# A selective-scan block on one core: which engine copies out the last states of the staged pairs

## The chip, the core and the metric

The kernel runs on one core of one Trainium2 chip. The metric is the time of one execution on the device in microseconds (us), and the smaller it is the better. The engines are called by their names in the profile: PE is TensorE, DVE is VectorE, ACT is ScalarE, POOL is GpSimd and SP is SyncE. PEld is the weight load of TensorE.

## The reference

A Mamba block and then a mixture of experts work on 8 x 1024 tokens of width 256, both on layer-normed inputs with residual sums. The part that matters here is the selective scan: 512 channels, each with 16 states, and a first-order recurrence over time for each of them.

```python
def step(s, inp):
    d_t, B_t, C_t, u_t = inp
    dA = jnp.exp(d_t[..., None] * A)
    dBu = d_t[..., None] * B_t[:, None, :] * u_t[..., None]
    s = dA * s + dBu
    y_t = jnp.einsum('bdn,bn->bd', s, C_t)
    return (s, y_t)
s0 = jnp.zeros((Bsz, Di, N), dtype=u.dtype)
_, ys = lax.scan(step, s0, xs)
```

After it the top 2 of 8 experts are applied to each token and the result is layer-normed. All values are fp32.

## The kernel before, in words

The first part of the kernel (to about 1785 us of the trace) is the Mamba block with the routing, the second part the experts. Only the first is touched.

**Tiling.** The 8192 tokens are 16 chunks (NC) of 512 tokens (CH). A sequence of 1024 tokens is two chunks, so an even chunk starts its states at zero and the odd chunk behind it starts them from the last states of the even one. The 512 channels are four groups (G) of 128 partitions, and each group has 16 states (N). One scan is one instruction on DVE over 128 channels x 512 tokens for one state n. A chunk is thus 64 scans (SG), which the code counts as steps: step s of a chunk is group s // 16, state s % 16. Every engine has its own loop over the same steps, written out by hand, with tables that say at which step a projection, a routing piece or a copy is issued. Each engine runs its queue strictly in order and semaphores join the queues.

**One scan.** ACT makes the decay, an exp of 128x512 (`exp_a`, line 1215, the most frequent ACT instruction). POOL makes the drive of two states at once (`times_b`, line 902), except for state pairs 2 and 5 (`BMS`), where PE makes it (line 1508) and ACT writes the exp to `dbu`. DVE scans (line 763).

**Held and direct states.** States with n % 3 == 0 are *held*: their exp goes to the fifth PSUM bank, and their result goes to the SBUF tile `ss` (the profile calls it `area`, since it is a part of a larger tile). `ss` has two slots, each for one *staged* pair: states 0 and 3, 6 and 9, 12 and 15. So there are three staged pairs in each group, numbered s = 3t + j over all groups t (`STAGED` holds the first state of each). POOL weighs a staged pair by C (`weigh` of POOL, line 919) and PE adds it up. The other ten states are *direct* pairs; their scans stay in PSUM, DVE weighs them (line 775) and PE adds them up.

**Last states.** In even chunks the last column of each scan goes to the tile `carry`, from which the odd chunk starts. The five direct pairs are copied by ACT (`keep`, line 1222). Before the change the three staged pairs are copied by POOL (line 913), just before it weighs the pair. There are 8 even chunks x 4 groups x 3 pairs = 96 such copies of 128x2.

**What waits for what.** The exp of a held state waits until the scan of the held state before it is done (they share a bank), and the exp of a direct state waits for DVE's weighing of an earlier pair and, in even chunks, for that pair's `keep`. The scan of a staged pair s waits until POOL has weighed pair s - 2, which lay in the same slot. In every chunk, DVE's `add_dt` of group 2 (line 735) stands at step 10 and waits for ACT's `soft_log` (line 1184), which stands at step 12 of ACT's queue; between them at step 9 ACT has the gate's Silu with two table loads (line 1199). A second Silu stands at step 41 (line 1193).

Of the kernel before, what the change touches and what calls it, by code (L numbers as in the profile page):

```python
# [178 lines left out]
def mamba_block(nc, both, x_t, x1_t, b_dram, ln_g, ln_b, W_in, conv_w, conv_b, W_xproj, W_dt, b_dt, A_log, D_param,  # L179
# [29 lines left out]
    with ExitStack() as ctx:  # L209
# [3 lines left out]
        def sem(name):  # L213
            return ctx.enter_context(nc.semaphore(name))
# [85 lines left out]
        wd_turned = sem("turned_dve")  # L300
        wp_turned = sem("turned_pool")
        carry_act = sem("carry_act")
        carry_pool = sem("carry_pool")
        gated = sem("gated")
        made = sem("masks_made")
        lnr_step = sem("routed_ln_step")
# [47 lines left out]
        SCATTER_END = NC * G * HB + 1  # L354
        DIAGONALS = (54, 57, 61, 63)
        DRIVE = (4, 4, 10, 10)
        KEEP_EARLY = (4, 9)
        EARLY_AT = [CUTS[0] * SG + at for at in (47, 48, 50, 51)] + [(CUTS[0] + 1) * SG + at for at in range(46, 54)] + [
            c * SG + 47 for c in CUTS[1:]]
# [85 lines left out]
        def kept(k):  # L445

            c, g, n = k // SG, k // N % G, k % N
            return ND * (G * (c // 2) + g) + product(n) + 1

        def routed(q, j):  # L450

# [159 lines left out]
        def _(dve):  # L611
# [126 lines left out]
            def scan(c, g, n):  # L738
                t = c * G + g
                k = t * N + n  # L740
                if n // 2 in BMS:
                    dve.wait_ge(tb_done, driven(t, n))
                elif n % 2 == 0:
                    dve.wait_ge(dbu_done, products(t, n // 2))
                dve.wait_ge(exp_done, k + 1)
                if held(n):

                    s = 3 * t + n // 6
                    if n in STAGED and s >= 2:
                        dve.wait_ge(wp_done, s - 1)  # L750
                    dst = ss[:, s % 2, n // 3 % 2, :]
                else:
                    dst = ps_a[:, bank(k), :]
                init = 0.0
                if c % 2:
                    init = carry[:, g, n:n + 1]
                    if held(n):
                        dve.wait_ge(carry_pool, 3 * (G * (c // 2) + g) + n // 6 + 1)
                    else:
                        dve.wait_ge(carry_act, kept(k))  # L760
                pair = ps_a[:, bank(k), :], dbu[:, k // 2 % NBU, n % 2, :]
                decay, drive = reversed(pair) if n // 2 in BMS else pair
                dve.tensor_tensor_scan(dst, decay, drive, init, ALU.mult, ALU.add).then_inc(scan_done, 1)  # L763
# [82 lines left out]
        def _(pool):  # L846
# [58 lines left out]
            def weigh(t, j):  # L905

                c, g = t // G, t % G
                n = STAGED[j]
                rows = slice(n, n + 4, 3)
                s = 3 * t + j  # L910
                pool.wait_ge(scan_done, t * N + n + 4)
                if c % 2 == 0:
                    pool.tensor_copy(carry[:, g, rows], ss[:, s % 2, :, CH - 1]).then_inc(carry_pool, 1)
                if s >= 2:
                    pool.wait_ge(wp_turned, s - 1)
                if g == 0:
                    for m in {n // 2, (n + 3) // 2}:
                        pool.wait_ge(c_in[m], 16 * (c + 1))
                pool.tensor_tensor(wp[:, s % 2], ss[:, s % 2], cc[:, rows, :], ALU.mult  # L919
                                   ).then_inc(wp_done, 1)  # L920
# [40 lines left out]
        def _(act):  # L961
# [262 lines left out]
            def follows(k):  # L1224

                return next(j for j in range(k + 1, k + N) if bank(j) == bank(k))

            keep_at = {}
            for t in range(NC * G):
                if t // G % 2 == 0:  # L1230
# [60 lines left out]
            for at in range(STEPS):  # L1291
                c, s = divmod(at, SG)
                if s == HALO_AT and c + 1 < NC:
                    set_halo(c + 1)
                if s == XL_AT and 0 < c < NC:
                    residual_base(c - 1)
                if at == XL_LAST:
                    residual_base(NC - 1)
                for kind, g, q in empty_at.get(at, ()):
                    if kind == "dt":  # L1300
                        soft_abs(q, g)
                    else:
                        empty(kind, g, q)
                for kind, g, q in empty_at.get(at - 1, ()):
                    if kind == "dt":
                        soft_exp(q, g)
                for kind, g, q in empty_at.get(at - 2, ()):
                    if kind == "dt":
                        soft_log(q, g)
                if s in TAPS_ACT and c + 1 < NC:  # L1310
                    tap_product(c + 1, (3, 0, 1, 2)[TAPS_ACT.index(s)])
                if s == SILU_U and c + 1 < NC:
                    silu_u(c + 1)
                    act.preload_act_table_set("natural_log_exp_and_others")
                q = due(at, SILU_Z, 1)
                if q is not None:
                    silu_gate(q)
                    act.preload_act_table_set("natural_log_exp_and_others")
                for j, offset in enumerate(INV_STD):
                    q = due(at, offset, 2)  # L1320
                    if q is not None:
                        inv_std(q, j)
                for j, offset in enumerate(STATS_X1):
                    q = due(at, offset, -1)
                    if q is not None and q < NC - 1:
                        stats_x1(q, j)
                for j, offset in enumerate(INV_STD_X1):
                    q = due(at, offset, -1)
                    if q is not None and q < NC - 1:
                        inv_std_x1(q, j)  # L1330
                if s in NORM and c + 2 < NC:
                    normalise(c + 2, range(2) if s == NORM[0] else range(2, NT))
                if s in XN and 0 < c < NC:
                    normalise_x1(c - 1, range(2) if s == XN[0] else range(2, NT))
                for j, offset in enumerate(EXP_W):
                    q = due(at, offset, -1)
                    if q is not None and q < NC - 1:
                        weight_exp(q, j)
                for j, offset in enumerate(START_DIAGONALS):
                    if at == offset:  # L1340
                        diagonals(0, 2 + j)
                for j, offset in enumerate(DIAGONALS):
                    q = due(at, offset, 1)
                    if q:
                        diagonals(q, j)
                for k, offset in enumerate((IDS_0, IDS_1)):
                    q = due(at, offset, -1)
                    if q is not None and q < NC - 1:
                        row_meta(q, k)
                if c < NC:  # L1350
                    for k in keep_at.get(at, ()):
                        keep(k)
                    exp_a(c, s // N, s % N)

        @block.tensor
# [995 lines left out]
```

## Time and profile before

| | |
|---|---|
| median of 3 runs | 2302.48 us (2300.59 to 2304.11) |
| profiled execution, its own time | 2301.22 us |
| its span, first to last instruction | 2299.4 us |
| TensorE clock granted, mean | 0.971 of full speed |
| busy share of PE, DVE, ACT, POOL | 92%, 88%, 73%, 86% |

The shares are means over both parts of the kernel; in the scan part DVE is busier than in the experts. An "idle before" in a timeline row, in square brackets, is the time that the engine stood still ahead of that row and what ended it.

### The profile page before, as it was taken

The numbers are of one execution on the slowest core, as the hardware profiler recorded it, in microseconds if no ns is written. First come the engines' busy times: TensorE is split into PE (matmuls) and PEld (weight loads), VectorE is DVE, ScalarE is ACT, GpSimd is POOL, SyncE is SP. The second block draws the span as 40 slices with busy tenths as digits, with TensorE's granted clock in tenths as the row PEclk, the third lists the DMA queues.
The fourth block names the chain that finished last, engine by engine and source line by source line (L and its number), as shares of the span: only waits on it lengthen the run. The fifth ranks groups of instructions, "written<-read, shape, count | busy, mean of one in ns | idle before, by whom it ended". The sixth has DMA issues, their size and how long they took to land. (4 is left out here: it accounts for less than half of the span.)

```text
span 2299.4 us, 45508 instructions
## 1 busy us (share of the span) xinstructions
PE 2116.1 (92%) x13263; PEld 1725.8 (75%) x13263; DVE 2034.8 (88%) x2843; ACT 1685.7 (73%) x3447; POOL 1971.4 (86%) x1252
## 2 busy tenths in 40 slices
PE   8889899999989898989898989999978999999996
PEld 5667677777767676767777777777767899999885
DVE  5999999999999999999999999999999556657776
ACT  6787879788888888877778787888765444445664
POOL 3988999999999899989899999989898467667775
PEclk9999999999999999999999999999998999999998
DMA  5041414233241415050514142323325667657886
GB/s 189 3 157 47 148 52 152 68 126 110 86 141 56 165 37 173 23 174 27 168 39 156 52 146 71 130 91 104 102 84 181 135 125 156 131 97 165 182 181 153
DMA packets 226007, 263.59 MB, mean 115 GB/s; under 512 B 101123, under 2 KB 182563, under 8 KB 225636
## 3 DMA queue, kind: packets, MB, share of 16 engines
q1 hardware_dynamic: 175172, 208.07, 29.0%
q0 software_dynamic: 29904, 34.77, 8.3%
q10 hardware_dynamic: 20688, 17.85, 2.5%
q8 instruction: 111, 1.82, 0.3%
q14 instruction: 132, 1.08, 0.2%
HBM read 196.75 MB, written 71.71 MB: 117 GB/s over the span
## 5 line engine op out<-in xcount | busy, mean ns | idle before, releaser
L902 POOL TENSOR_TENSOR dbu<-drive_u,w_all 128x1024 f32<-128x1024 f32 x384 | 904.1, 2365 | 61.2 <-DVE ps_a L763 43.4
L1215 ACT ACTIVATE ps_a<-delta,a_neg 128x512 f32<-128x512 f32 x768 | 518.4, 685 | 117.8 <-DVE area L763 103.0
L919 POOL TENSOR_TENSOR wp<-area 128x1024 f32<-128x1024 f32 x192 | 453.2, 2360 | 8.5 <-DVE area L763 7.8
L775 DVE TENSOR_TENSOR wd<-ps_a,area 128x1024 f32<-128x1024 f32 x320 | 383.0, 1197 | 0.0
L1481 PEld LDWEIGHTS ps_y<-ident,wd 128*128 128x128 f32 x2560 | 309.3, 146 | 97.7 <-issue 72.1
L1481 PE MATMUL ps_y<-ident,wd 128*128 128x128 f32 x2560 | 347.1, 282 | 13.0 <-DVE wd L775 13.0
L2064 POOL DMA_INDIRECT acc_scratch<-ow,e_meta x135 | 221.2, 1639 | 132.8 <-DVE ow L1975 122.7
L1508 PEld LDWEIGHTS ps_a<-dg,duT 128*128 128x128 f32 x2048 | 255.1, 201 | 67.0 <-issue 65.0
L1508 PE MATMUL ps_a<-dg,duT 128*128 128x128 f32 x2048 | 265.5, 285 | 38.3 <-ACT carry L1222 36.0
L2306 PEld LDWEIGHTS e_ps_h<-xT,w_tile 128*128 128x128 f32 x2160 | 259.6, 192 | 16.9 <-DVE xT L1953 10.5
L2306 PE MATMUL e_ps_h<-xT,w_tile 128*128 128x128 f32 x2160 | 265.5, 276 | 2.7 <-DVE xT L1953 1.9
L2316 PE MATMUL e_ps_o<-area,e_hT 128*128 x1080 | 255.6, 379 | 0.4 <-DVE e_hT L1960 0.4
L763 DVE TENSOR_TENSOR_SCAN area<-ps_a,carry,dbu 128x512 f32<-128x512 f32 x192 | 242.0, 1260 | 1.5 <-issue 1.5
L763 DVE TENSOR_TENSOR_SCAN ps_a<-ps_a,carry,dbu 128x512 f32<-128x512 f32 x192 | 237.6, 1271 | 0.4 <-issue 0.4
L763 DVE TENSOR_TENSOR_SCAN area<-ps_a,dbu 128x512 f32<-128x512 f32 x192 | 230.4, 1200 | 5.2 <-ACT ps_a L1215 5.0
L763 DVE TENSOR_TENSOR_SCAN ps_a<-ps_a,dbu 128x512 f32<-128x512 f32 x192 | 225.9, 1211 | 4.9 <-ACT ps_a L1215 4.9
L1491 PE MATMUL ps_y<-ident,wp 128*128 128x128 f32 x1536 | 215.1, 286 | 9.6 <-POOL wp L919 9.5
L2316 PEld LDWEIGHTS e_ps_o<-area,e_hT 128*128 128x128 f32 x1080 | 194.9, 190 | 21.7 <-issue 0.8
L2113 ACT ACTIVATE e_hT<-e_ps_h,b_turned 128x128 f32<-128x128 f32 x270 | 84.9, 364 | 170.9 <-PE e_ps_h L2306 167.3
L1491 PEld LDWEIGHTS ps_y<-ident,wp 128*128 128x128 f32 x1536 | 187.2, 149 | 23.0 <-POOL wp L919 14.1
L2105 ACT COPY w_tile<-w_all 128x1024 f32 x135 | 141.0, 1045 | 57.6 <-issue 51.5
L1389 PE MATMUL ps_p<-area 128*128 128x512 f32 x368 | 178.0, 593 | 0.8 <-ACT area L1096 0.8
(248 smaller groups left out, 3842.1 us busy)
## 6 DMA issues: line engine op xcount, KB each, us to landing
area<-b_scratch SPq DMA_DIRECT2D x128, 512.0 KB, 4.8
w_all<-b_scratch SPq DMA_DIRECT2D x96, 512.0 KB, 3.9
dg<-xs_scratch SPq DMA_DIRECT2D x540, 32.0 KB
area<-in_L_attn_x_dram SPq DMA_DIRECT2D x32, 512.0 KB, 4.9
ee<-acc_scratch SPq DMA_DIRECT2D x32, 512.0 KB, 4.0
x_scratch<-area SPq DMA_DIRECT2D x16, 512.0 KB, 2.9
acc_scratch<-area SPq DMA_DIRECT2D x16, 512.0 KB
area<-x_scratch ACTq DMA_DIRECT2D x32, 256.0 KB
```

What stands on the lines that cost most here:

```text
L763: dve.tensor_tensor_scan(dst, decay, drive, init, ALU.mult, ALU.add).then_inc(scan_done, 1)
L775: dve.tensor_tensor(wd[:, s % NWD], states(k, 2), cc[:, n:n + 2, :], ALU.mult).then_inc(wd_done, 1)
L902: pool.tensor_tensor(dbu[:, k % NBU], du[:, g % 2, :].unsqueeze(1).broadcast_to([P, 2, CH]), bb[:, row:row + 2, :], ALU.mult).then_inc(dbu ...
L919: pool.tensor_tensor(wp[:, s % 2], ss[:, s % 2], cc[:, rows, :], ALU.mult).then_inc(wp_done, 1)
L1215: act.activation(dst, dl[:, g, :], ACT.Exp, scale=a_neg[:, g, n:n + 1]).then_inc(exp_done, 1)
L1389: ins = pe.matmul(dst, taps[:, g, k, :], xin[:, g, k:k + CH], start=(k == 0), stop=(k == TAPS - 1))
L1481: ins = pe.matmul(ps_y[:, i, :], wd[:, s % NWD, h, i * P:(i + 1) * P], ident[:], start=False, stop=False, is_transpose=True, skip_group_ch ...
L1491: ins = pe.matmul(ps_y[:, i, :], wp[:, s % 2, h, i * P:(i + 1) * P], ident[:], start=False, stop=(j == 2 and h == 1 and i == NT - 1), is_t ...
L1508: ins = pe.matmul(ps_a[:, bank(k), i * P:(i + 1) * P], duT[:, i, :], dg[:, p, h, i, :], start=True, stop=True)
L2064: pool.indirect_dma_start(out=acc_dram, out_offset=bass.IndirectOffsetOnAxis(ap=meta[:, old, 1:].bitcast(U32), axis=0), in_=ow[:, old, :], ...
L2306: ins = pe.matmul(inner(1 - par, j), w1s[:, 1 - par, k, j * P:(j + 1) * P], xT[:, 1 - par, :, k, :], start=(k == 0), stop=(k == KD - 1))
L2316: ins = pe.matmul(ps_o[:, par, 0:D], hT[:, par, k, :], w2[:, bass.ds((e * KF + k) * D, D)], start=(k == 0), stop=(k == KF - 1))
```

## The change

ACT copies out the last states of the three staged pairs, instead of POOL. The copy of the pair that starts at state n is issued at step n + 6 of the same group (for n = 12 that is step 2 of the next group), ahead of that step's exp. A new semaphore `carry_held` takes the place of `carry_pool`. The scan that writes a slot of `ss` again, two staged pairs later, now waits for ACT's copy too, since POOL's weighing no longer implies it.

```diff
-        carry_pool = sem("carry_pool")
+        carry_held = sem("carry_held")
...
+        KEEP_HELD = 6
...
+        def copied(s):
+            return 3 * (G * (s // (3 * G) // 2) + s // 3 % G) + s % 3 + 1
...
                     if n in STAGED and s >= 2:
                         dve.wait_ge(wp_done, s - 1)
+                        if (s - 2) // 3 // G % 2 == 0:
+                            dve.wait_ge(carry_held, copied(s - 2))
...
                     if held(n):
-                        dve.wait_ge(carry_pool, 3 * (G * (c // 2) + g) + n // 6 + 1)
+                        dve.wait_ge(carry_held, 3 * (G * (c // 2) + g) + n // 6 + 1)
...
                 pool.wait_ge(scan_done, t * N + n + 4)
-                if c % 2 == 0:
-                    pool.tensor_copy(carry[:, g, rows], ss[:, s % 2, :, CH - 1]).then_inc(carry_pool, 1)
...
+            def keep_held(s):
+
+                t, n = s // 3, STAGED[s % 3]
+                act.wait_ge(scan_done, t * N + n + 4)
+                act.copy(carry[:, t % G, n:n + 4:3], ss[:, s % 2, :, CH - 1]).then_inc(carry_held, 1)
+
+            held_at = {s // 3 * N + STAGED[s % 3] + KEEP_HELD: s for s in range(3 * NC * G) if s // (3 * G) % 2 == 0}
...
                     for k in keep_at.get(at, ()):
                         keep(k)
+                    if at in held_at:
+                        keep_held(held_at[at])
                     exp_a(c, s // N, s % N)
```

In the rows below a name in square brackets is a semaphore: `scan_done` and `weighed_dve` come from DVE, `carry_act` from ACT's `keep`, `proj_full` from PE. The lines of the changed kernel stand four or more further down (1215 becomes 1219, 1222 becomes 1226, 1136 becomes 1140); the new copy is line 1236.

**ACT, start of an even chunk.** This is ACT's queue of the kernel before from step 3 to the first table load of step 9 of chunk 6:

```order
963 L1215 ACTIVATE ps_a<-delta,a_neg 128x512 [waits scan_done]
964 L1215 ACTIVATE dbu<-delta,a_neg 128x512 [waits scan_done] x2
965 L1091 ACTIVATE area<-ps_p,lnb,lng 128x512 [waits proj_full]
966 L1215 ACTIVATE ps_a<-delta,a_neg 128x512 [waits scan_done]
967 L1222 COPY carry<-ps_a 128x2 [waits weighed_dve]
968 L1215 ACTIVATE ps_a<-delta,a_neg 128x512 [waits carry_act,weighed_dve] x2
969 L1136 COPY area<-ps_p 128x4x128 [waits proj_full]
970 L1199 ACT_TABLE_LOAD [waits proj_evacuated1,proj_evacuated0]
```

The same place in the changed kernel reads:

```order
1003 L1219 ACTIVATE ps_a<-delta,a_neg 128x512 [waits scan_done]
1004 L1219 ACTIVATE dbu<-delta,a_neg 128x512 [waits scan_done] x2
1005 L1095 ACTIVATE area<-ps_p,lnb,lng 128x512 [waits proj_full]
1006 L1236 COPY carry<-area 128x2 [waits scan_done]
1007 L1219 ACTIVATE ps_a<-delta,a_neg 128x512 [waits scan_done]
1008 L1226 COPY carry<-ps_a 128x2 [waits weighed_dve]
1009 L1219 ACTIVATE ps_a<-delta,a_neg 128x512 [waits carry_act,weighed_dve] x2
1010 L1140 COPY area<-ps_p 128x4x128 [waits proj_full]
1011 L1203 ACT_TABLE_LOAD [waits proj_evacuated1,proj_evacuated0]
```

The copy of states 0 and 3 stands ahead of the exp of step 6 and waits on `scan_done`, as that exp does; the exp does not wait for the copy.

**ACT, start of an odd chunk.** This is ACT's queue of the changed kernel from step 1 to step 5 of chunk 5; the kernel before has the same rows without line 1236:

```order
851 L1219 ACTIVATE ps_a<-delta,a_neg 128x512 [waits carry_act,weighed_dve]
852 L1140 COPY area<-ps_p 128x4x128 [waits proj_full]
853 L1104 COPY area<-ps_p 128x512 [waits proj_full]
854 L1236 COPY carry<-area 128x2 [waits scan_done]
855 L1219 ACTIVATE ps_a<-delta,a_neg 128x512 [waits carry_act,weighed_dve]
856 L1095 ACTIVATE area<-ps_p,lnb,lng 128x512 [waits proj_full]
857 L1219 ACTIVATE ps_a<-delta,a_neg 128x512 [waits scan_done]
```

Here the copy is the one of states 12 and 15 of the last group of the even chunk ahead, at step 2.

**POOL.** This is POOL's queue of the kernel before in the first groups of an even chunk:

```order
198 L913 COPY carry<-area 128x2
199 L919 TENSOR_TENSOR wp<-area 128x1024
200 L889 TENSOR_TENSOR drive_u<-delta,xc 128x512
201 L902 TENSOR_TENSOR dbu<-drive_u,w_all 128x1024
202 L876 DMA xs_scratch<-area,sli 67456x258
203 L902 TENSOR_TENSOR dbu<-drive_u,w_all 128x1024 x2
204 L913 COPY carry<-area 128x2
205 L919 TENSOR_TENSOR wp<-area 128x1024
```

In the changed kernel the two rows of line 913 are gone, and nothing else on this queue has moved.

## Rows read from the trace of the kernel before

**Rows 1.** The page, part 1: busy time of each engine, share, instructions.
```profile
PE 2116.1 (92%) x13263; PEld 1725.8 (75%) x13263; DVE 2034.8 (88%) x2843; ACT 1685.7 (73%) x3447; POOL 1971.4 (86%) x1252
```

**Rows 2.** Busy time of each engine in a 200 us window of the scans.
```profile
400.00:600.00 200.00, 185.56 (x1154) 143.88 (x1153) 194.97 (x215) 166.84 (x348) 189.65 (x112) 0.98 0.33 112
```

**Rows 3.** Waits of DVE, 110 to 1760 us: total us, times, longest.
```profile
DVE delta L735 <- ACT delta L1184: 22.9, 15, 1.8
DVE ps_a L763 <- PE ps_a L1508: 13.1, 15, 1.6
```

**Rows 4.** Waits of POOL, the same stretch, the longest.
```profile
POOL dbu L902 <- DVE ps_a L763: 41.1, 43, 2.4
```

**Rows 5.** The tile carry: POOL's copies, duration in ns min/median/max.
```profile
L913 POOL COPY carry<-area x96: 177/192/250, 50.6 to 1673.7; 128x2 f32<-128x2 f32 x96
```

**Rows 6.** Timeline of ACT: small copies and what starts behind them.
```profile
578.28 0.20 ACT L969 ACTIVATE area<-area 128x12 uint32<-128x12 uint32 x1
578.38 0.56 ACT L1100 COPY area<-ps_p 128x512 f32<-128x512 f32 x1
...
584.75 0.17 ACT L1222 COPY carry<-ps_a 128x2 f32<-128x2 f32 x1
584.79 1.35 ACT L1215 ACTIVATE dbu<-delta,a_neg 128x512 f32<-128x512 f32 x2
```

**Rows 7.** Timeline of chunk 6, ACT and then DVE.
```profile
694.09 0.69 ACT L1215 ACTIVATE ps_a<-delta,a_neg 128x512 f32<-128x512 f32 x1
694.75 0.16 ACT L1222 COPY carry<-ps_a 128x2 f32<-128x2 f32 x1
695.01 1.30 ACT L1215 ACTIVATE ps_a<-delta,a_neg 128x512 f32<-128x512 f32 x2
696.25 0.57 ACT L1136 COPY area<-ps_p 128x512 f32<-128x512 f32 x1
...
693.53 1.19 DVE L775 TENSOR_TENSOR wd<-ps_a,area 128x1024 f32<-128x1024 f32 x1
...
707.38 0.69 DVE L735 SCALAR_TENSOR_TENSOR delta<-ps_p,delta 128x512 f32<-128x512 f32 x1 [1.75 <-ACT delta L1184]
```

**Rows 8.** ACT at step 9 of chunks 4 and 14, first and last of four.
```profile
482.73 0.59 ACT L1136 COPY area<-ps_p 128x512 f32<-128x512 f32 x1 [0.48 <-PE ps_p L1450]
...
1571.24 0.59 ACT L1136 COPY area<-ps_p 128x512 f32<-128x512 f32 x1 [0.47 <-PE ps_p L1450]
```

**Rows 9.** Timeline of chunk 5 at step 9, ACT and then PE.
```profile
586.70 1.92 ACT L1215 ACTIVATE ps_a<-delta,a_neg 128x512 f32<-128x512 f32 x3
588.68 0.59 ACT L1136 COPY area<-ps_p 128x512 f32<-128x512 f32 x1
...
588.01 0.63 PE L1450 MATMUL ps_p<-ident,area 128*128 128x128 f32 x4 [0.70 <-DVE area L785]
```

**Rows 10.** Timeline at step 41 of chunk 4, ACT and then DVE.
```profile
535.36 1.07 ACT L1120 COPY area<-ps_p 128x512 f32<-128x512 f32 x2 [0.18 <-PE ps_p L1405]
...
538.97 0.19 DVE L643 TENSOR_REDUCE mx<-ps_p 128x4 f32<-128x32 f32 x1 [0.38 <-PE ps_p L1413]
```

**Rows 11.** Timeline of DVE, chunk 0 at step 9.
```profile
60.17 1.22 DVE L763 TENSOR_TENSOR_SCAN area<-ps_a,dbu 128x512 f32<-128x512 f32 x1 [1.84 <-ACT ps_a L1215]
```

**Rows 12.** Windows at step 41 of chunks 2 and 4; DVE's wait in chunk 2.
```profile
324.00:326.00 2.00, 2.00 (x11) 2.00 (x10) 1.97 (x5) 1.99 (x4) 1.34 (x1) 0.50 0.01 4
539.00:541.00 2.00, 2.00 (x18) 1.73 (x17) 2.00 (x4) 1.97 (x3) 0.87 (x2) 1.00 0.00 0
...
330.98 2.34 DVE L763 TENSOR_TENSOR_SCAN ps_a<-dbu,ps_a 128x512 f32<-128x512 f32 x2 [1.59 <-PE ps_a L1508]
```

**Rows 13.** Timeline of POOL at one copy, and DVE's scan beside it.
```profile
521.19 0.18 POOL L913 COPY carry<-area 128x2 f32<-128x2 f32 x1
521.33 2.35 POOL L919 TENSOR_TENSOR wp<-area 128x1024 f32<-128x1024 f32 x1
...
520.22 1.20 DVE L763 TENSOR_TENSOR_SCAN area<-ps_a,dbu 128x512 f32<-128x512 f32 x1
```

## The prediction, made before the changed kernel ran

> **What bounds the kernel now.** I read the page first. PE has the largest share and POOL 86%, with 1971.4 us [rows 1]; that alone would say that work taken off POOL is worth something. But the shares are means over two parts, so I then took the windows of the scan part. In 200 us of it DVE is busy 194.97 us, POOL 189.65, PE 185.56 and ACT 166.84 [rows 2]. DVE stands still about 5 us, and the question is only what ends those waits. The list of DVE's waits from 110 to 1760 us answers it: 22.9 us, 15 times, for ACT's `soft_log` of line 1184, and 13.1 us, 15 times, for a drive made by PE (line 1508) [rows 3]. No wait of DVE in that list is ended by POOL. The list of POOL's waits shows the opposite direction: POOL stands 41.1 us in 43 places for DVE's scans, at the drives of line 902 alone [rows 4]. So POOL is nearly full, but it follows DVE; DVE is the bound, and where DVE waits, the end of the wait comes out of ACT or PE.
>
> The timelines show the two chains behind those waits. In every chunk DVE stands at `add_dt` of group 2, for 1.75 us in chunk 6 [rows 7]. What it waits for is ACT, which from step 3 on runs without a gap through exps, copies, Silu and two table loads. A longer ACT queue ahead of that point makes DVE's wait longer, unless ACT itself has a gap on the way. So the price of the change is decided by where the 96 copies fall against ACT's gaps, and not by ACT's 73%.
>
> **What the change removes.** POOL loses 96 copies with a median of 192 ns [rows 5], 18.4 us of busy time. The next instruction starts 0.14 us behind a copy's start (521.19 to 521.33) [rows 13], so its queue is 96 x 0.14 = 13.4 us shorter. DVE never waits for POOL [rows 3], and what POOL gains becomes a longer wait for DVE's scans in the places of [rows 4]. Gain: 0. The cover is DVE itself; if it went, the gain would be up to 13.4 us.
>
> **What the change adds to ACT.** 96 copies from SBUF of two elements. The trace has no such copy on ACT, so I bound it by three rows. An SBUF to SBUF operation of 12 elements takes 0.20 us and the next one starts 0.10 us behind its start [rows 6]: this is nearest, and I take c = 0.10. The cheapest is a `keep` with nothing behind it that waits for it, 0.04 us (584.75 to 584.79) [rows 6]. The dearest is a `keep` between two exps of which the second waits for it: from exp to exp 694.09 to 695.01 is 0.92 us [rows 7], and two exps without it are 0.62 apart (from 695.01, two exps and then line 1136 at 696.25 [rows 7]), so 0.30. The rows of the new order show that the exp behind the new copy has no wait on it, which is why I don't take 0.30, but it stays the upper end.
>
> The copy's own wait is free. At steps 6 and 12 it waits for the scan for which that step's exp waits anyway, and at step 2 of the next group it waits for the last scan of the group, for which the exp of step 0 has waited already. No ACT instruction is held by a wait that it did not have.
>
> **What the change adds to DVE.** The scan of staged pair s waits for the copy of s - 2. That copy stands in ACT's queue four to six steps ahead of this scan's own exp, and the scan has always waited for that exp. So the wait is over before it is reached: 0.
>
> **Which of the copies count.** A copy costs time only where ACT runs from it to one of DVE's waits without a gap. Twelve copies fall in each even chunk; I go through the places.
> - Chunks 2, 6 and 8, step 6: no gap to `soft_log`. But the `keep` behind it starts at 694.75, when DVE's weighing ends (693.53 + 1.19 = 694.72), which is 0.66 us behind the exp ahead instead of 0.62 [rows 7]. That slack of 0.04 takes a part: 3 x (0.10 - 0.04) = 0.18 us.
> - Chunks 4, 10, 12 and 14, step 6: ACT stands 0.48 or 0.47 us at step 9 for PE (line 1450) [rows 8]. The copy disappears in it: 0, also at 0.30.
> - Odd chunks (8 of them), step 2: three exps start at 586.70, so ACT could start line 1136 at 586.70 + 3 x 0.62 = 588.56, and it starts at 588.68 because PE's transposes end at 588.01 + 0.63 = 588.64 [rows 9]. They hang on DVE's gate. The slack is 0.12: 0, and at 0.30 it is 8 x 0.18 = 1.4 us.
> - Chunk 0, step 6: DVE waits 1.84 us for ACT behind the table loads [rows 11], without slack: 1 x 0.10.
> - Steps 34 and 38 of the seven even chunks from 2 on: two copies ahead of the second Silu, and ACT's only gap there is 0.18 us; behind it stands the logit matmul, for which DVE waits 0.38 us [rows 10]. 7 x (0.20 - 0.18) = 0.14 us.
> - The other copies are followed by one of ACT's waits for a DVE scan before anything of DVE's depends on them: 0.
>
> Sum: 0.18 + 0 + 0 + 0.10 + 0.14 = **0.4 us slower**. With c = 0.04 it is 0 + 0 + 0 + 0.04 + 0 = 0.04, and with c = 0.30 it is 3 x 0.26 + 1.4 + 0.3 + 7 x 0.42 = 5.4 us.
>
> The sum stands against the profiled execution's own time, 2301.2 + 0.4 = 2301.6 us. That execution is 1.3 us below the median of the three runs, so for the median I forecast 2302.48 + 0.4 = **2302.9 us**. About 0.2% (4.6 us) is what a measurement of this kernel can tell from no change.
>
> **The rivals.**
> - *POOL's relief counts.* If POOL's lateness reached DVE in a way that the waits don't show, up to 13.4 us would go: 2289 us. For it speaks that POOL is 189.65 of 200 us busy [rows 2]. Against it, that no wait of DVE ends with POOL [rows 3] and that POOL waits so often itself [rows 4]. A second way is contention in SBUF: if DVE stood for as long as POOL's copies take, 18.4 us would go, 2284 us. The scan that wholly contains a copy (520.22 to 521.42, the copy at 521.19) takes 1.20 us [rows 13], and the scans with a zero start take 1.19 to 1.22 in the rows that I read, copy or not. Together 0.07.
> The Trainium skill has a rule that speaks for this rival: GPSIMD Engine Reference, Specifications, says that GpSimd's SBUF interfaces are shared with VectorE and that instructions with two SBUF inputs contend. By that rule a scan or a weighing here is not such an instruction, as its names in the rows give one input in PSUM (`ps_a`) and one in SBUF, and the trace agrees, with 1.20 us beside a copy.
> - *The copy drains ACT.* Slower: each copy costs the whole bracket of 0.30 us at the places above. The result would be +5.4 us, 2307.9 us. It passes 0.2% from c = 0.27 on (26c - 2.4 = 4.6, with 3 + 8 + 1 + 14 = 26 copies and 2.4 us of slack). For it speaks the `keep` at the same step, which does cost that; against it, that nothing waits for the new copy, and the 0.04 of the `keep` at 584.75 [rows 6]. 0.07.
> - *The clock falls elsewhere.* In chunks 2, 6, 8 and 14, but not in 4, 10 and 12, DVE waits another 1.6 us at step 42 (1.59 in chunk 2), and there the granted TensorE clock is 0.50 (its 1.2 GHz level) just before, against 1.00 (2.4 GHz) in chunk 4, though PE is busy in both [rows 12]. A shift of some tenths may move that: from 4 x 1.6 = 6.4 us faster to 3 x 1.6 = 4.8 us slower, 2296.5 to 2307.7 us. The order has little to do with it, so most of this lies within 0.2%. 0.06.
> - *The forecast*: 0.80.
>
> **The numbers.** The forecast's own range is 0.04 to 1 us over before, with the spread of the runs (2300.6 to 2304.1) about it. The range reaches down for some of the clock's cases and up towards the drained copy: 2299.0 to 2307.0 us. Faster by over 0.2%: 0.07, nearly all from the first rival. Slower: 0.08, 0.06 from the drained copy and 0.02 from the clock. Within 0.2%: 0.85.
>
> **What would show it right or wrong.** POOL's busy time should fall by some 18 us to 1953 and its waits for DVE's scans grow by some 13. ACT should have 96 copies at line 1236 with about 0.2 us each, and the next instruction 0.10 us behind. DVE's wait for `soft_log` should stay at 22.9 us to within 1 us, and no wait of DVE should name `carry`. Line 1136 in chunks 4, 10, 12 and 14 should have its idle time of 0.48 cut to about 0.38. I am wrong if DVE's scans or weighings have become shorter than before, if DVE's waits for PE have fallen with POOL's work, or if ACT's copy costs 0.3.

## The result, and the profile after

The changed kernel takes 2302.96 us (median of 20 runs, 2298.16 to 2305.70). The kernel before, run beside it as often, takes 2298.59 us (2293.83 to 2304.11). The ratio is 1.0018, 95% interval 1.0012 to 1.0025: slower by 4.4 us, just under the 0.2% of the prediction. Of the three runs that were known ahead, two (2302.48 and 2304.11) lie above all 17 later ones of that kernel and the third (2300.59) above most. So the forecast of 2302.9 us hit the number by luck: its base was 3.9 us too high, and its step of 0.4 us was 4.0 us too small.

The two profiled executions hide this. They took 2301.22 and 2301.63 us, 0.4 us apart, because single executions of one kernel differ by several us. The busy row after the change answers to [rows 1]:

```profile
PE 2116.6 (92%) x13263; PEld 1725.2 (75%) x13263; DVE 2036.9 (89%) x2843; ACT 1692.9 (74%) x3543; POOL 1957.2 (85%) x1156
```

POOL lost 14.2 us of its 1971.4 and ACT gained 7.2, as wanted. DVE, which should not have changed at all, is busy for 2.1 us more with the same 2843 instructions. The waits from 110 to 1760 us (total, times, longest) answer to [rows 3] and [rows 4]:

```profile
DVE delta L739 <- ACT delta L1188: 22.9, 15, 1.8
DVE ps_a L769 <- PE ps_a L1521: 11.9, 13, 1.6
...
POOL dbu L908 <- DVE ps_a L769: 46.9, 46, 2.4
...
POOL wp L923 <- DVE area L769: 15.7, 19, 2.1
```

DVE's wait for `soft_log` is the same to the tenth, and POOL's waits for DVE have grown (its weighings waited 7.2 us in the kernel before, and its copies 3.6). The list of waits thus doesn't show the loss, and DVE's instructions have to be looked at one by one. One of them stands out. In chunk 10 DVE tests which expert tiles have started, one 128x8 instruction at scan 47. Timelines of POOL and then DVE there, first before the change:

```profile
1209.78 0.19 POOL L913 COPY carry<-area 128x2 f32<-128x2 f32 x1
1209.92 2.36 POOL L919 TENSOR_TENSOR wp<-area 128x1024 f32<-128x1024 f32 x1
1212.25 2.36 POOL L902 TENSOR_TENSOR dbu<-drive_u,w_all 128x1024 f32<-128x1024 f32 x1
...
1210.75 1.39 DVE L621 BATCH_NORM_STATS2 st<-area 128x6 f32<-128x256 f32 x4
1212.06 0.25 DVE L679 SCALAR_TENSOR_TENSOR tile_started<-seen,tile_row,region_base 128x8 f32<-128x8 f32 x1
```

and after it:

```profile
1206.23 2.37 POOL L923 TENSOR_TENSOR wp<-area 128x1024 f32<-128x1024 f32 x1
1208.55 2.36 POOL L908 TENSOR_TENSOR dbu<-drive_u,w_all 128x1024 f32<-128x1024 f32 x1
...
1208.51 2.43 DVE L683 SCALAR_TENSOR_TENSOR tile_started<-seen,tile_row,region_base 128x8 f32<-128x8 f32 x1
```

Before, the test began 0.19 us ahead of POOL's drive and was done in 0.25 us, 0.03 us behind the end of the weighing (1209.92 + 2.36 = 1212.28). After, it began 0.04 us ahead of the drive, 0.09 us before the weighing ended (1206.23 + 2.37 = 1208.60), and it ended at 1210.94, with the drive (1208.55 + 2.36 = 1210.91). Its inputs `seen` and `region_base` are both in SBUF. The batch statistics just ahead have one SBUF input and run beside POOL's weighing without any delay. Chunk 14 shows the same hold, across two POOL instructions (after the change):

```profile
1643.34 2.37 POOL L923 TENSOR_TENSOR wp<-area 128x1024 f32<-128x1024 f32 x1
1645.66 2.36 POOL L908 TENSOR_TENSOR dbu<-drive_u,w_all 128x1024 f32<-128x1024 f32 x1
...
1644.11 3.94 DVE L683 SCALAR_TENSOR_TENSOR tile_started<-seen,tile_row,region_base 128x8 f32<-128x8 f32 x1
```

It ends at 1648.05, POOL at 1648.02. The Trainium skill, SBUF — State Buffer, section SBUF: two separate sides, says that GpSimd and VectorE share one pair of SBUF ports as an exclusive lock, which a VectorE instruction in a 2-port perf mode or with two SBUF inputs needs, and that whichever starts first has it for its whole length. The trace agrees that DVE is shut out, with 3.94 us for 8 elements per partition. By the recorded starts it doesn't show who gets the pair at a change from one POOL instruction to the next, since in chunk 10 the drive got it although the test was issued 0.04 us earlier.

Two inputs are not the whole condition here. In chunk 8 of before a 128x8 instruction with a single SBUF tensor as input is held in the same way, until POOL's drive ends (987.08 + 2.35 = 989.43, against 989.47):

```profile
987.08 2.35 POOL L902 TENSOR_TENSOR dbu<-drive_u,w_all 128x1024 f32<-128x1024 f32 x1
...
986.71 2.76 DVE L685 TENSOR_SCALAR base_full<-region_base 128x8 f32<-128x8 f32 x1
```

In the last experiment it is moved to the start of chunk 0. There it takes 0.16 us in the one kernel, where POOL stands still at that time, and 2.11 us in the other, until POOL's drive ends (45.49 + 2.11 = 47.60, against 45.22 + 2.35 = 47.57). Whether it runs in such a perf mode no run here shows.

The theories to be tested:
- **Port theory**: some DVE instructions are held until POOL's instruction beside them has ended. POOL's queue without its copy of 0.14 us stands differently against DVE. The test in chunk 10 misses its opening and costs 2.2 us.
- **Copy theory**: the 4 us are ACT's time in the 96 copies.
- **Drift theory**: such long durations wander from one execution to the next.

### The profile page after: what moved, and what is told of

Read it like the earlier page. It is cut to its first block and busy times, and to the rows that moved or that the text cites. A ratio compares the mean times of both kernels' runs of the same rounds, so it can differ in the third digit from the quotient of the medians.

```text
span 2299.7 us, 45682 instructions
## 1 busy us (share of the span) xinstructions
PE 2116.6 (92%) x13263; PEld 1725.2 (75%) x13263; DVE 2036.9 (89%) x2843; ACT 1692.9 (74%) x3543; POOL 1957.2 (85%) x1156
```

## A measure with less noise

DVE's waits of 1.1 to 1.6 us for PE's drive, of which the clock rival spoke, do wander: there are 7 and 5 of them in two profiles of before, and 3 to 9 in the others. So for each profile I take DVE's stretch from the `soft_log` wait in chunk 0 to that in chunk 15, and subtract the waits of over 1 us for that drive. I call the rest the *net stage*. Its two ends, before and then after:

```profile
66.64 0.69 DVE L735 SCALAR_TENSOR_TENSOR delta<-ps_p,delta 128x512 f32<-128x512 f32 x1 [2.99 <-ACT delta L1184]
...
1691.81 0.69 DVE L735 SCALAR_TENSOR_TENSOR delta<-ps_p,delta 128x512 f32<-128x512 f32 x1 [0.90 <-ACT delta L1184]
```

```profile
64.73 0.69 DVE L739 SCALAR_TENSOR_TENSOR delta<-ps_p,delta 128x512 f32<-128x512 f32 x1 [1.19 <-ACT delta L1188]
...
1691.22 0.69 DVE L739 SCALAR_TENSOR_TENSOR delta<-ps_p,delta 128x512 f32<-128x512 f32 x1 [0.91 <-ACT delta L1188]
```

Before: 1625.2 less 7 waits of 9.8 us in all is 1615.4. After: 1626.5 less 6 waits of 8.2 is 1618.3. The net stage of a kernel comes from its one profile; two profiles of one kernel differ by 0.4 us (before) and 0.6 us (after), and what wanders ahead of chunk 0's wait is not in it. The table has everything that was measured: the median, the ratio to the kernel before as it ran beside this one (its medians there are 2298.59, 2298.05 or 2297.87, so ratios compare better than medians), the net stage, and the test in chunk 10:

| kernel | median us | ratio (95%) | net stage us | test in chunk 10, us |
|---|---|---|---|---|
| before | 2298.59 | | 1615.4 | 0.25 |
| before again | 2297.28 | 1.0000 (0.9990 to 1.0010) | 1615.8 | 0.26 |
| after | 2302.96 | 1.0018 (1.0012 to 1.0025) | 1618.3 | 2.43 |
| after again | 2302.62 | 1.0016 (1.0007 to 1.0025) | 1618.9 | 2.44 |
| both copies | 2299.55 | 1.0004 (0.9995 to 1.0013) | 1618.2 | 0.27 |
| no copies | 2299.20 | 1.0007 (0.9996 to 1.0017) | 1616.3 | 2.46 |
| ACT's copies twice | 2303.95 | 1.0026 (1.0017 to 1.0035) | 1621.9 | 2.44 |
| copies behind `keep` | 2298.87 | 1.0002 (0.9993 to 1.0010) | 1616.3 | 2.43 |
| after, test of chunk 10 moved | 2299.78 | 1.0005 (0.9996 to 1.0014) | 1615.6 | 0.19 |
| after, four tests moved | 2293.36 | 0.9973 (0.9964 to 0.9983) | 1612.0 | 0.19 |
| before, four tests moved | 2292.86 | 0.9978 (0.9968 to 0.9988) | 1609.8 | 0.20 |
| behind `keep`, four moved | 2291.18 | 0.9973 (0.9963 to 0.9983) | 1609.5 | 0.19 |
| before, all moved | 2287.54 | 0.9957 (0.9943 to 0.9970) | 1605.4 | 0.20 |
| behind `keep`, all moved | 2282.59 | 0.9936 (0.9921 to 0.9950) | 1604.4 | 0.19 |

## The experiments

**Before again.** No edit.

> The kernel before, unchanged, so that a second profiled execution of it exists. Every theory: ratio 1.000 (0.9993 to 1.0007). Port theory (a DVE instruction with two SBUF inputs is held until the GpSimd instruction beside it has ended): in this profile the test of the started tiles in chunk 10, which took 0.25 us in the first profile of before (at 1212.06), again lasts about 0.25 us, because GpSimd comes to the same seam at the same time; in chunks 12 and 14 it lasts 2.7 and 4.1 us as before. Drift theory (such waits and the half-clock waits wander by chance between executions): it lasts 0.2 us in one execution and 2.4 us in another of the same kernel.

Ratio 1.0000. The test lasts 0.26 us again (0.25 in the first profile), and POOL's drive begins 0.18 us behind it:

```profile
1206.28 0.26 DVE L679 SCALAR_TENSOR_TENSOR tile_started<-seen,tile_row,region_base 128x8 f32<-128x8 f32 x1
...
1206.46 2.36 POOL L902 TENSOR_TENSOR dbu<-drive_u,w_all 128x1024 f32<-128x1024 f32 x1
```

Its wandering waits are 5, not 7, and its span is 5.8 us shorter: 3.2 us by these waits and 3.5 us ahead of the net stage, which begins at 63.12 and not at 66.64. So they wander, and the test doesn't.

**After again.** No edit.

> The changed kernel, unchanged, for a second profiled execution. Both theories of a real loss: ratio 1.0018 (1.0010 to 1.0026). Port theory: the test of the started tiles in chunk 10 lasts 2.4 us again (first profile of after: 2.43). Copy theory (what is lost is ScalarE's time in the copies): that instruction may last either 0.2 or 2.4 us and the time is 1.0018 all the same.

Ratio 1.0016, and 2.44 us in the test, with the drive 0.06 us behind it (1210.40 and 1210.46):

```profile
1210.40 2.44 DVE L683 SCALAR_TENSOR_TENSOR tile_started<-seen,tile_row,region_base 128x8 f32<-128x8 f32 x1
...
1210.46 2.36 POOL L908 TENSOR_TENSOR dbu<-drive_u,w_all 128x1024 f32<-128x1024 f32 x1
```

The drift theory falls for the test. The loss is real, since it came out twice.

**Both copies.** The place for `spare` comes from `base_full`, which now shares one with another 128x8 tile; that and the new semaphore are left out here.

```diff
+        spare = sb("spare", [P, 2])
...
+                if c % 2 == 0:
+                    pool.wait_ge(spared, copied(s) - 1)
+                    pool.tensor_copy(spare[:], ss[:, s % 2, :, CH - 1]).then_inc(spared, 1)
                 if s >= 2:
                     pool.wait_ge(wp_turned, s - 1)
```

> The changed kernel, with GpSimd's copies put back beside ScalarE's: GpSimd copies the same two last states per pair into a small spare tile that nobody reads (room for it comes from letting two 128x8 tiles of the tile table share one place). ScalarE's copies stay the ones that are used. Port theory: GpSimd stands against DVE as in the kernel before, the test of the started tiles in chunk 10 falls from 2.43 to about 0.25 us, and the time goes back by about 2.2 us to a ratio of 1.0008 (only ScalarE's own price of 0.4 to 0.6 us, and what is not explained, is left). Copy theory: ScalarE's copies are all still there, so the ratio stays at 1.0018 or above. Third possibility, GpSimd's copies cost something themselves: above 1.0025.

More work than in either kernel, and 3.1 us faster than after again. The test has its opening back: POOL's copy stands at 1209.90, the drive at 1212.36 and the test 0.19 us ahead of it, with 0.27 us:

```profile
1212.17 0.27 DVE L685 SCALAR_TENSOR_TENSOR tile_started<-seen,tile_row,region_base 128x8 f32<-128x8 f32 x1
```

The median supports the port theory. The net stage doesn't: it is that of after (1618.2 against 1618.3 and 1618.9), though the test gave 2.2 us back. Of these, 0.5 us went into four other held instructions in chunks 8, 12 and 14, which are 0.12 to 0.14 us longer each than after the change. I can't place the rest.

**After, four tests moved.**

```diff
-            c * SG + 47 for c in CUTS[1:]]
+            c * SG + 46 for c in CUTS[1:]]
```

> The changed kernel, with the test of the started tiles (one 128x8 instruction on DVE with two SBUF inputs) in chunks 10, 12, 14 and 15 one scan earlier, at scan 46 of the chunk instead of scan 47, where GpSimd sits in the issue of its indirect stores and runs no arithmetic. Port theory: the four instructions fall from 2.43, 2.63, 3.94 and 0.22 us to about 0.2 us each, DVE gets back 8.4 us, of which next to all lies on the path since DVE waits for little there: 2303.0 - 8.4 = 2294.6 us, a ratio to the kernel before of 0.998 (0.9965 to 0.9995). Rival (the long durations are a record of something DVE would wait for anyway, such as the drive of the next scan or the clock): the time goes back into the next wait and the ratio stays at 1.0018.

2293.36 us, 9.6 below after. All four tests take 0.19 to 0.20 us, and 6.3 to 6.9 us of the net stage go (from 1618.3 and 1618.9 to 1612.0). POOL and DVE in chunk 10:

```profile
1204.61 1.01 POOL L882 DMA_INDIRECT xs_scratch<-area,sli  x1 [1.24 <-DVE sli L671]
1205.92 0.96 POOL L882 DMA_INDIRECT xs_scratch<-area,sli  x1 [0.30 <-issue]
...
1205.63 0.19 DVE L683 SCALAR_TENSOR_TENSOR tile_started<-seen,tile_row,region_base 128x8 f32<-128x8 f32 x1
```

The rival, that the time would go back into the next wait, falls for the greater part. The four tests became 8.4 us shorter and the net stage 6.3 to 6.9. In chunk 14 a part came back as a wait, for nothing that the profile names, which neither profile of after has:

```profile
1639.26 1.23 DVE L769 TENSOR_TENSOR_SCAN area<-ps_a,dbu 128x512 f32<-128x512 f32 x1 [1.13 <-issue]
```

**Before, four tests moved.** The same edit in the kernel before.

> The kernel before, with the test of the started tiles in chunks 10, 12, 14 and 15 at scan 46 of the chunk instead of 47. Its four instructions last 0.25, 2.75, 4.07 and 0.22 us in the profiles of before. Port theory: they fall to 0.2 us each, DVE gets back 6.4 us, so 2298.6 - 6.4 = 2292.2 us, ratio 0.9972; what is then left between this kernel and the changed one with the same move (2293.4) is the real price of having the copies on ScalarE rather than on GpSimd, 0 to 1.5 us. Copy theory (the 4 us between after and before are ScalarE's time): this kernel has to come out 4 us below the changed one with the same move, at 2289.4 us, ratio 0.996.

2292.86 us. The copy theory wanted 2289.4 by the median, which did not come; the net stages, 1609.8 and 1612.0, leave 2.2 us between the two kernels where no test is held. By the net stage that is the price of the copies on ACT, more than I had allowed (0 to 1.5). The medians don't show it: they are 0.5 us apart, and the ratios lean the other way (0.9978 and 0.9973), well within their intervals.

**No copies.** The edit takes out line 913 and the scans' wait for it, and adds:

```diff
+            dve.memset(carry[:], 0.0)
```

> The kernel before, without the 96 copies of held last states on any engine: neither GpSimd nor ScalarE makes them, and the scans of those pairs in the odd chunks start from zero, which DVE writes into the tile once at the start. That part of the computation is left out. GpSimd is then as short as in the changed kernel, and ScalarE as short as in the kernel before. Port theory: GpSimd reaches chunk 10 as in the changed kernel, the test of the started tiles there lasts 2.4 us instead of 0.25, and the time is that of the changed kernel less ScalarE's 0.5 to 1 us: ratio 1.0014 (1.0005 to 1.0022), slower than before though work was only taken away. Copy theory: nothing is left that could cost anything, ratio 1.000 or below. Relief theory (GpSimd's copies held the kernel up): 0.994 (13.4 us less).

This kernel leaves out the last states of the staged pairs: those scans start at zero in the odd chunks too. Its ratio is 1.0007 with an interval that holds 1: the median decides nothing. The profile does: POOL without copies, ACT as before, and the test lasts 2.46 us. So it is POOL's missing 0.14 us that makes the test miss, and nothing on ACT. The net stage is 0.5 to 0.9 us over before, not 2.2. DVE gets a part back: four other held instructions are 0.12 to 0.15 us shorter each, as the POOL copy in their way is gone (3.95 against 4.08 in chunk 14), and its other waits are 0.7 us less (30.8 against 31.5). The relief theory falls.

**ACT's copies twice.** `spare` is made as in the kernel with both copies.

```diff
                 act.wait_ge(scan_done, t * N + n + 4)
+                act.copy(spare[:], ss[:, s % 2, :, CH - 1])
                 act.copy(carry[:, t % G, n:n + 4:3], ss[:, s % 2, :, CH - 1]).then_inc(carry_held, 1)
```

> The changed kernel, with each of ScalarE's 96 copies made twice, the first time into a small spare tile that nobody reads. Port theory with a small price of a copy: one more copy of 0.08 to 0.10 us costs what the first does at the places that are not covered, 0.4 to 1.4 us in all, so ratio 1.002 (1.0017 to 1.0025). Copy theory: the 96 copies cost 4 us, so 96 more cost at least 4 us again: ratio 1.0035 or above. The test of the started tiles in chunk 10 stays at 2.4 us by both.

1.0026. The median is 1.0 to 1.3 us over after's and the ratio 0.8 to 1.0 thousandths (1.8 to 2.3 us), at the upper edge of what the port theory had (1.0025) and below the copy theory's 1.0035. The net stage grows by 3.0 to 3.6 us, more than the 0.4 to 1.4 expected. One place shows the price of one copy. At step 26 of the even chunks DVE waits for PE's drive; in chunk 4 of before, after and twice:

```profile
517.97 1.23 DVE L763 TENSOR_TENSOR_SCAN ps_a<-dbu,ps_a 128x512 f32<-128x512 f32 x1 [0.44 <-PE ps_a L1508]
```

```profile
513.97 1.23 DVE L769 TENSOR_TENSOR_SCAN ps_a<-dbu,ps_a 128x512 f32<-128x512 f32 x1 [0.53 <-PE ps_a L1521]
```

```profile
516.12 1.23 DVE L770 TENSOR_TENSOR_SCAN ps_a<-dbu,ps_a 128x512 f32<-128x512 f32 x1 [0.63 <-PE ps_a L1523]
```

0.09 and 0.10 us for each copy, without any cover, at a place that I had put among those that cost nothing. The same wait stands in all seven even chunks from 2 on: 0.44 us in before, 0.53 or 0.54 in after, 0.63 with the copies twice. Chunk 0, which has no such wait in before, has one of 0.37 and 0.56 us in the two profiles of after and of 0.71 us with the copies twice.

**Copies behind `keep`.**

```diff
-            held_at = {s // 3 * N + STAGED[s % 3] + KEEP_HELD: s
+            held_at = {s // 3 * N + STAGED[s % 3] + (7, 7, 5)[s % 3]: s
```

> The changed kernel, with each of ScalarE's copies of held last states behind a copy of last states that ScalarE makes anyway, in one step with it, so that its time lies in the 0.25 us that the next exponential waits for there: pairs 0 and 6 one step later (seven scans after the pair's first), pair 12 one step earlier (five after). Port theory: GpSimd's work is as in the changed kernel, the test in chunk 10 stays at 2.4 us, and only ScalarE's uncovered share goes, 0.4 to 0.6 us: ratio 1.0015 (1.0006 to 1.0022). Copy theory: with the copies hidden the time falls back to that of before, ratio 1.000. Rival to both: two copies in a row drain ScalarE for longer, 1.002 or above.

1.0002, against the 1.0015 that the port theory gave, and the net stage is that of the kernel without copies (1616.3): here the 96 copies cost nothing. The wait at step 26 is 0.44 us again in the seven chunks, and gone in chunk 0. The median is 3.8 to 4.1 us under after's, of which the net stage explains 2.0 to 2.6. (The profiled execution was the slowest of the twelve, 2307.08 us, with 9 of the wandering waits.) The port theory alone was wrong about this, and the ratio is the one that the copy theory gave: where the copies stand on ACT is about as large a part of the loss as the test.

**After, test of chunk 10 moved.**

```diff
-            c * SG + 47 for c in CUTS[1:]]
+            c * SG + 47 - (c == 10) for c in CUTS[1:]]
```

> The changed kernel, with the test of the started tiles one scan earlier in chunk 10 alone; in chunks 12, 14 and 15 it stays at scan 47. It lasts 2.43 us in chunk 10 in the profiles of after. Port theory: 0.2 us in chunk 10, 2.6 and 3.9 us in chunks 12 and 14 as before, chunk 10 itself takes 106.5 to 106.8 us from its wait for delta to the next one's instead of 108.8, and the time falls by about 2.2 us, to a ratio of 1.0008 (1.0000 to 1.0015). Copy theory: the copies are all there and 1.0018 stays.

2299.78 us, 2.8 to 3.2 under after, and chunk 10 takes 106.7 us instead of 108.8. That shows what this one instruction costs: 2.1 us there.

**Behind `keep`, four tests moved.** The last two edits together, the tests in all four chunks.

> Both moves that helped by themselves: ScalarE's copies behind the copies of last states that it makes anyway, and the test of the started tiles in chunks 10, 12, 14 and 15 at scan 46. If ScalarE's copies cost time only by where they stand, the scan stage without its half-clock waits is that of the kernel before with the same move of the test (1609.8 us from chunk 1 to chunk 15), against 1612.0 in the changed kernel with the move, and the time is 2292.5 us (2290 to 2295), ratio 0.9975. If the copies cost the same wherever they stand: 1612 us again.

As expected: net stage 1609.5, that of before with the same move (1609.8). Against 1612.0 with the copies at step n + 6 it is 2.5 us, of which 2.3 fall in the eight even chunks, 0.8 in chunk 0 alone. The ratios of these two kernels are equal (0.9973), with intervals of 1 thousandth to each side, so this gain stands on the net stage alone.

**All tests moved**, in the kernel before and in the one with the copies behind `keep`. `base_full`, the held instruction with one input, goes to step 1 of chunk 0, chunk 8's two tests and chunk 9's first four table steps to scan 46. The waits that go with this, and the loop that lets several steps stand at one scan, are left out here:

```diff
-        EARLY_AT = [CUTS[0] * SG + at for at in (47, 48, 50, 51)] + [(CUTS[0] + 1) * SG + at for at in range(46, 54)] + [
-            c * SG + 47 for c in CUTS[1:]]
+        EARLY_AT = [1] + [CUTS[0] * SG + 46] * 3 + [(CUTS[0] + 1) * SG + at for at in (46, 46, 46, 46, 50, 51, 52, 53)] + [
+            c * SG + 46 for c in CUTS[1:]]
```

> The kernel before, with every small DVE instruction that was held moved to where GpSimd runs no arithmetic: the test of the started tiles in chunks 10, 12, 14 and 15 to scan 46 as in the run before; in chunk 8 both tests at scan 46, with the tile that they need computed once in chunk 0; in chunk 9 the first four steps of the tile table at scan 46 in a row, where they waited or were held for 1.25 and 1.97 us. Port theory: beside the 6.4 us of chunks 10 to 15 the 2.76, 0.85 and 2.38 us of chunk 8 and the 1.25 and 1.97 us of chunk 9 fall to about 0.2 each: another 8 us, so 2298.0 - 5.2 - 8 = 2285 us, ratio 0.994 (0.9930 to 0.9955), unless what DVE gains in chunks 8 and 9 goes into waits for drives that GpSimd makes; then 0.9965.

> The same moves in the changed kernel with ScalarE's copies behind the copies that it makes anyway. It tells what the change itself is worth once GpSimd holds nobody up and ScalarE's copies are out of the way. If GpSimd's 96 copies never mattered: the same time as the run before, within 2 us. If GpSimd's relief counts once DVE has become faster: 2 to 6 us less than that, ratio 0.992 to 0.993.

0.9957 and 0.9936. The second is the best kernel here, 15.3 us faster than the kernel before that ran beside it. In the first, 4.4 us of the net stage went, not 8. Chunk 8 is 5.5 us shorter, but chunk 9 gained nothing: a product in the tile table that had been free (0.23 us) is now held, since DVE comes to it earlier, inside POOL's weighing:

```profile
1099.43 3.27 DVE L708 TENSOR_TENSOR early_jump<-early_passed,early_jump 128x8 f32<-128x8 f32 x1
...
1099.08 2.37 POOL L919 TENSOR_TENSOR wp<-area 128x1024 f32<-128x1024 f32 x1
1101.40 1.27 POOL L889 TENSOR_TENSOR drive_u<-delta,xc 128x512 f32<-128x512 f32 x1
```

Again it ends with POOL (1102.70 and 1102.67); the second kernel has the same hold, of 3.00 us. A DVE wait of 1.72 us in chunk 10, for nothing that the profile names, is in this kernel and not in the other. The two medians are 5.0 us apart, with six runs each; their net stages 1.0. The expectation of 2 to 6 us for POOL's relief came out in the medians and not in the net stages, so whether POOL's relief itself counts for something now is not settled.

## Why the prediction was right or wrong

**POOL's relief is worth nothing**: right. No copies at all brought no gain. POOL's busy time fell by 14.2 us and not by 18.4: a copy's record of 0.19 us overlaps the next instruction, which starts 0.14 us behind it, and the busy share counts such time once. I should have used the 13.4 us of the queue for both. POOL's waits for DVE's scans grew by 10.9 us (63.0 to 73.9), against the 13 of the prediction.

**DVE's new wait is free, and `soft_log` stays at 22.9**: right. No wait names `carry`.

**The price of one copy, c = 0.10**: right. In chunk 10 of after the next exp starts 0.08 us behind it, and 0.09 to 0.10 reached DVE.

```profile
1210.54 0.18 ACT L1236 COPY carry<-area 128x2 f32<-128x2 f32 x1
1210.62 0.68 ACT L1219 ACTIVATE ps_a<-delta,a_neg 128x512 f32<-128x512 f32 x1
```

**Which of the copies count**: this step failed. "The other copies are followed by one of ACT's waits for a DVE scan before anything of DVE's depends on them: 0." I followed ACT to DVE directly, and not through PE. But DVE's scans wait for drives of PE, and PE's drives wait for ACT's `keep`, 38.0 us in all, as the page of after says in its groups:

```profile
L1521 PE MATMUL ps_a<-dg,duT 128*128 128x128 f32 x2048 | 262.4, 283 | 41.0 <-ACT carry L1226 38.0
```

That total shows the link and not the price: it is 36.0 us in before, 38.7 in after again, 37.6 without any copies and 37.4 behind `keep`, where the copies cost nothing. The price shows in DVE's waits at step 26, which end with PE's drive: 7 x 0.09 us and the 0.37 to 0.56 of chunk 0 are 1.0 to 1.2 us. The whole term was 0.4 us in the prediction; it measured 2.0 to 2.6 us in the net stage. Chunk 0, with 0.10 in the sum, cost 0.5 to 0.8 in most profiles (102.7 to 102.9 us without copies at step n + 6, 103.3 to 103.5 with them) and 0.2 in one. How the delay arises there, and by which way the part beyond step 26 reaches DVE, was not followed link by link.

**The gap of 0.48 us in chunks 4, 10, 12 and 14** [rows 8]: half right. I expected it at 0.38. In one profile of after it is 0.43 in chunk 4, in the other it is gone:

```profile
478.65 0.58 ACT L1140 COPY area<-ps_p 128x512 f32<-128x512 f32 x1
```

The windows ahead of that place, of before and then of this profile (the third value from the right is the granted clock):

```profile
476.00:481.00 5.00, 5.00 (x31) 4.94 (x32) 5.00 (x6) 4.91 (x10) 4.80 (x4) 0.66 0.69 197
```

```profile
472.00:477.00 5.00, 4.67 (x40) 4.42 (x40) 5.00 (x6) 5.00 (x10) 4.81 (x4) 1.00 0.67 192
```

The cover stood where PE ran at its lower level (1.2 GHz) for a part of that window, 0.66 against 1.00. It doesn't come from the order of the instructions: chunk 6, with no such gap in before, has one of 0.47 us in before again and of 0.43 in the first profile of after.

**Contention in SBUF**: this is the second step that failed. I asked about it only as a gain. I looked at the scans and weighings, found that they are not held (1.20 us beside a copy, right), and left out the small instructions that work on SBUF alone, some of them 2 to 4 us long in the trace of before. So the sum lacked a term of +2.2 us in chunk 10, less 0.5 us for four holds that became 0.12 to 0.15 us shorter.

Together, with parts that come from different kernels: 2.2 - 0.5 + 2.3 (the even chunks with the tests moved) - 0.7 (DVE's other waits, as in the kernel without copies) = 3.3 us, and the net stages of after and before differ by 2.5 to 3.5 us (1618.3 and 1618.9 against 1615.4 and 1615.8). The medians differ by 4.4. The rest lies in the wandering waits or outside the stage, and I can't place it. Nor do the parts add up in the medians: the test of chunk 10 alone gave back 3 us, the place of the copies alone 4, and the intervals of 0.9 to 1 thousandth (2.1 to 2.3 us) are too wide to say how much of that is chance.

**The clock rival**: it does move single executions, and no part of the 4.4 us was shown to come from it. **The drained copy** (0.30 us each) was not seen.

So the forecast lay inside its range for the wrong reason. It said that almost nothing would change, and two costs of about 2 us each, neither of them in its sum, came out just under the 0.2% that it had set as its limit.

## What to carry to other kernels

Taking work off an engine that nobody waits for still moves its instructions against the others. List the instructions whose duration in the trace is many times that of their like and ends with an instruction of another engine, here small DVE instructions that work on SBUF alone beside a busy POOL, and put them where POOL issues a DMA or waits; a 128x8 instruction can cost 4 us. And follow a delay through every engine: an addition to ACT that no DVE wait names can reach DVE through PE.

## What the runs showed of the hardware

- A DVE instruction of 128x8 with two SBUF inputs takes 0.15 to 0.23 us when free and up to 4.1 us beside POOL arithmetic; in the timelines above it then ends within 0.03 us of a POOL instruction's end. A 128x8 `TENSOR_SCALAR` with one SBUF input took 2.11 to 2.77 us beside POOL arithmetic and 0.16 us free. Batch statistics with one SBUF input (1.39 us for four) are not held.
- Whether it gets through where one POOL instruction follows another is repeatable but not simple. It got through when it began 0.18 or 0.19 us ahead of the next one (three profiles, 0.25 to 0.27 us, ending 0.03 to 0.04 us behind the one ahead), and not at 0.04 and 0.06 us, nor in chunk 12 of before at 0.37 us (1426.36 and 1426.73). In chunk 14 it was held past such a place, for 3.9 to 4.1 us. What decides it wasn't found.
- A kernel that makes each copy twice, on POOL and on ACT, was 3.1 us faster by its median than the one that makes it once, on ACT.
